# Copying the first batch's split q and k from SBUF straight to the stacks, and moving batch 1's projections and split ahead of other start-up work, in a fused adaLN, attention and mixture-of-experts kernel

## The reference: what is computed

```python
mod = (_silu(L0_c) @ L0_wmod).reshape(L0_c.shape[0], 6, 1, -1)
sa, ca, ga, sb, cb, gb = (mod[:, 0], mod[:, 1], mod[:, 2], mod[:, 3], mod[:, 4], mod[:, 5])
ga = (2 * (ga >= 0) - 1) * jnp.maximum(jnp.abs(ga), 0.25)   # gb in the same way
h = _layernorm(x, axis=-1) * (1 + ca) + sa
x = x + ga * _L0_attn_ref(h, ...)      # 16 heads of width 8, softmax over 256 keys
h = _layernorm(x, axis=-1) * (1 + cb) + sb
x = x + gb * _L0_ffn_ref(h, ...)       # 14 experts, one (the argmax) for each token
```

## Time and profile before

| what | value |
|---|---|
| median of 3 runs | 626.4 us (625.49 to 626.9) |
| the profiled execution, from its first to its last instruction | 626.1 us |
| PE, DVE, ACT, POOL busy | 476.2, 552.7, 543.4, 498.0 us |
| granted PE clock, mean | 0.637 |

### The profile page before, as it was taken

The page is one execution under the profiler, slowest core; times in us unless marked ns, Lnnn a source line. Parts: engine busy times, 40 slices in busy tenths (PEclk is TensorE's granted clock), DMA queues, the critical chain, the costliest instruction groups (busy, mean ns, idle before and its releaser), DMA issues.

```text
span 626.1 us, 11856 instructions
## 1 busy us (share of the span) xinstructions
PE 476.2 (76%) x2529; PEld 269.8 (43%) x2531; DVE 552.7 (88%) x1430; ACT 543.4 (87%) x2310; POOL 498.0 (80%) x655
## 2 busy tenths in 40 slices
PE   5457877887687888787777788788766868989880
PEld 2123333433333333343333344344332548878870
DVE  5899899999999999999999999999999787868660
ACT  2599999999999999999999999999999656757650
POOL 4466777898998999998998989899887664777774
PEclk9556566556756655556656655655655588999886
DMA  6365555555555545554445555655553126676640
GB/s 193 106 184 144 135 136 141 148 149 146 155 151 146 155 139 144 147 148 137 143 135 144 152 158 172 182 164 162 146 156 111 50 90 183 189 205 190 194 124 1
DMA packets 75432, 91.66 MB, mean 146 GB/s; under 512 B 12925, under 2 KB 59043, under 8 KB 75359
## 3 DMA queue, kind: packets, MB, share of 16 engines
q1 hardware_dynamic: 66826, 72.93, 43.6%
q0 software_dynamic: 6560, 16.83, 7.2%
q10 hardware_dynamic: 1976, 1.15, 0.7%
HBM read 58.41 MB, written 33.29 MB: 146 GB/s over the span
## 4 chain that ended last, share of the span: by engine, by line
ACT 47%; POOL 17%; DVE 13%; PE 8%; issue 8%; DMA 5%; ACTq 1%; POOLq 0%; DVEq 0%; SPq 0%
ACT scores L785 46%; DVE neg_max L1218 4%; POOL table L710 3%; PE scores L1052 3%; DMA x_s<-table 2%; POOL xhat L659 2%; PE scores L1061 2%; DMA out_dram<-out_room,ids_s 2%; POOL rstd L642 2%; POOL rest L478 1%; POOL parts L481 1%; POOL out_dram L761 1%; POOL h_scaled L682 1%; DVE w_e L1670 1%; POOL xhat L651 1%
## 5 line engine op out<-in xcount | busy, mean ns | idle before, releaser
L785 ACT ACTIVATE scores<-scores,neg_max 128x256 f32<-128x256 f32 x1024 | 468.5, 864 | 10.9 <-DVE neg_max L1218 10.7
L785 ACT ACTIVATION_READ_ACCUMULATOR scores<-scores,neg_max 128x1 f32 x1024 | 438.3, 624 | 0.0
L1218 DVE TENSOR_REDUCE neg_max<-scores 128x4 f32<-128x1024 f32 x256 | 309.1, 1211 | 6.7 <-PE scores L916 5.9
L916 PE MATMUL scores<-k_stack,q_stack 64*128 64x256 bf16 x1024 | 149.2, 390 | 80.8 <-ACT scores L785 69.2
L916 PEld LDWEIGHTS scores<-k_stack,q_stack 64*128 64x128 bf16 x1024 | 33.9, 106 | 166.1 <-ACT scores L785 121.3
L710 POOL DMA_INDIRECT table<-rows,place_i x64 | 66.1, 1033 | 19.9 <-issue 17.7
L761 POOL DMA_INDIRECT out_dram<-out_room,ids_s x65 | 65.8, 1013 | 19.8 <-issue 15.8
L817 ACT ACTIVATE hid<-scores,w_e 128x128 f32<-128x128 f32 x154 | 48.3, 365 | 22.2 <-PE scores L1052 21.2
L1052 PE MATMUL scores<-x_t,w_e 128*128 128x128 f32 x308 | 52.5, 297 | 1.7 <-ACT x_t L810 1.4
L659 POOL TENSOR_SCALAR xhat<-rows,mv,rstd 128x128 f32<-128x128 f32 x60 | 47.7, 797 | 7.1 <-POOL rstd L642 7.1
L1061 PE MATMUL scores<-w_s,hid 128*128 x308 | 50.1, 288 | 1.1 <-ACT hid L817 0.9
(11 more groups left out here) (178 smaller groups left out, 826.9 us busy)
## 6 DMA issues: line engine op xcount, KB each, us to landing
x_s<-table SPq DMA_DIRECT2D x77, 192.5 KB, 3.0
q_stack<-parts_dram SPq DMA_DIRECT2D x192, 64.0 KB, 2.9
parts_dram<-parts SPq DMA_DIRECT2D x31, 384.0 KB, 3.0
k_stack<-parts_dram SPq DMA_DIRECT2D x186, 64.0 KB, 2.3
mod_b<-mod_rows SPq DMA_DIRECT2D x32, 256.0 KB, 4.3
x_s<-in_x_dram SPq DMA_DIRECT2D x13, 256.0 KB, 4.7
w1x_s<-in_w1x_dram SPq DMA_DIRECT2D x7, 258.0 KB, 4.4
w_s<-in_w_dram SPq DMA_DIRECT2D x7, 256.0 KB, 4.5
```

Source lines behind the costliest of these rows:

```text
L785: last = act.activation(buf[:, k * L:k * L + L], buf[:, k * L:k * L + L], ACT.Exp, bias=neg_max[:, p, n:n + 1], accum_out=exp_sum[:, p, n: ...
L916: last = pe.matmul(scores[:, c, at:at + L], q_stack[p][r, g + j, t * P:t * P + P], k_stack[p][r, g + j, :], start=True, stop=True)
L1218: dve.tensor_reduce(to, scores[:, (PAIRS * b.n + i) % RING, :].rearrange("p (e j m) -> p e j m", e=2, j=2), AX_X, ALU.max, negate=True).th ...
```

## The change

Two things are changed. First, the parts of batch 0 no longer go through `parts_dram`. The new `load_first_by` copies one part of q or k from SBUF to each place of the stack that takes it: 9 DMAs from SP and 3 from ACT, each issued when its part is made. `first_k_stored` falls away, batch 2's split waits for all of stack 0 in its place, and the counts of `parts_stored` fall by one store. Second, the order at the start changes: PE runs the transposes and projections of batch 1 ahead of `late_mod`, DVE takes q and k of batch 1 ahead of `take_mod`, POOL splits batch 1 ahead of `root(3)` and `normalise_x(Batch(2))`, and DVE's `means` of batch 2 moves from ahead of `take_mod` to behind `modulate(0)`.

```diff
--- before.py
+++ after.py
@@ -369,7 +369,6 @@
         first_rest = sem("first_rest")
         first_middle = sem("first_middle")
         first_q_ready = sem("first_q_ready")
-        first_k_stored = sem("first_k_stored")
         b_qk_turned = sem("b_qk_turned")
         b_taken = sem("b_taken")
         w_moe_loaded = sem("w_moe_loaded")
@@ -469,9 +468,9 @@
 
             eng.wait_ge(qk_ready, b.done())
 
-            need(eng, parts_stored, 16 * b.n - 16)
             if b.n == 2:
-                eng.wait_ge(first_k_stored, 16)
+                eng.wait_ge(stacked[0], 16 * LOADS_STACK)
+            need(eng, parts_stored, 16 * b.n - 32)
             p = b.slot(2)
             steps.plain()
             steps.then(eng.tensor_copy(parts[:, p, :, 0, :], qk[:, :, :]))
@@ -488,6 +487,13 @@
                     src = parts_dram[p, side, part].rearrange("(c g) t -> c (g t)", g=HALF)
                     eng.dma_start(to[p][n:P:ROWS, :, :].rearrange("c g t -> c (g t)"), src).then_inc(stacked[p], 16)
 
+        def load_first_by(eng, side, part):
+
+            to, part_of = ((q_stack, Q_PART), (k_stack, K_PART))[side]
+            for n in range(COMBOS):
+                if part_of[n] == part:
+                    eng.dma_start(to[0][n:P:ROWS, :, :], parts[:, 0, side, part, :]).then_inc(stacked[0], 16)
+
         @block.sync
         def _(sp):
             steps = Steps(sp, sp_held, sp_held)
@@ -515,7 +521,7 @@
 
             def parts_landed(b):
 
-                sp.wait_ge(parts_stored, 16 * b.n + 16)
+                sp.wait_ge(parts_stored, 16 * b.n)
                 steps.plain()
 
             def pad_front(n):
@@ -527,11 +533,13 @@
             sp.wait_ge(pad_set, 2)
             pad_front(0)
             sp.wait_ge(stacks_set, 4)
+            for side in range(2):
+                sp.wait_ge(first_high, side + 1)
+                load_first_by(sp, side, 0)
+            sp.wait_ge(first_middle, 1)
+            load_first_by(sp, 0, 1)
             sp.wait_ge(first_q_ready, 1)
-            sp.dma_start(parts_dram[0, 0].rearrange("s r t -> r s t"), parts[:, 0, 0]).then_inc(parts_stored, 16)
-            sp.wait_ge(parts_stored, 16)
-            steps.plain()
-            load_stacks_by(sp, 0, (0,))
+            load_first_by(sp, 0, 2)
             store_parts(Batch(1))
             parts_landed(Batch(1))
             load_stacks_by(sp, 1, (0, 1))
@@ -713,9 +721,9 @@
             root(1)
             root(2)
             normalise_x(Batch(1))
+            split_by(pool, steps, Batch(1))
             root(3)
             normalise_x(Batch(2))
-            split_by(pool, steps, Batch(1))
             pool.wait_ge(w_in_loaded, 16 * LOADS_IN)
 
             def iteration(b):
@@ -858,10 +866,10 @@
             act.copy(first[1][:, 1, :], rest[:, 1, :]).then_inc(first_middle, 1)
             act.wait_ge(stacks_set, 4)
 
+            act.wait_ge(first_middle, 2)
+            load_first_by(act, 1, 1)
             act.wait_ge(parts_ready, 1)
-            act.dma_start(parts_dram[0, 1].rearrange("s r t -> r s t"), parts[:, 0, 1]).then_inc(first_k_stored, 16)
-            act.wait_ge(first_k_stored, 16)
-            load_stacks_by(act, 0, (1,))
+            load_first_by(act, 1, 2)
             over_batches(iteration, drain)
 
             over_tiles(tile, PRIMED, AT_W1)
@@ -985,10 +993,10 @@
             pe.wait_ge(h_ready, 1)
             pe.matmul(first_qk[0], w_qk_s[:, 0, :], h_t[0][:, :], start=True, stop=True).then_inc(first_q_done, 1)
             pe.matmul(first_qk[1], w_qk_s[:, 1, :], h_t[0][:, :], start=True, stop=True).then_inc(qk_done, 1)
-            late_mod()
             turn_x(Batch(1))
             project_q(Batch(1))
             project_k(Batch(1))
+            late_mod()
             pe.wait_ge(b_taken, 1)
 
             pe.wait_ge(mod_taken, 2)
@@ -1379,9 +1387,6 @@
                 dve.tensor_tensor(parts[:, 0, side, 2, :], rest[:, side, :], parts[:, 0, side, 1, :], ALU.subtract).then_inc(done, 1)
             make_h(Batch(1))
             stats_x(Batch(2))
-            dve.wait_ge(xhat1_ready, 2)
-            steps.plain()
-            means(True, False)
             dve.wait_ge(consts_set, SETS)
 
             def take_mod():
@@ -1418,11 +1423,14 @@
                 steps.then(dve.tensor_tensor(bias_out[:, 1, :], bias_f[:, 1, :], bias_f[:, 1, :], ALU.max))
                 dve.tensor_tensor(bias_out[:, 2, :], bias_f[:, 1, :], bias_out[:, 1, :], ALU.subtract).then_inc(bias_ready, 1)
 
+            take_qk(Batch(1))
             take_mod()
-            take_qk(Batch(1))
             dve.wait_ge(mod_taken, 2)
             steps.plain()
             modulate(0)
+            dve.wait_ge(xhat1_ready, 2)
+            steps.plain()
+            means(True, False)
             dve.wait_ge(w_in_loaded, 16 * LOADS_IN)
             dve.wait_ge(mod_taken, 2)
             dve.wait_ge(xhat1_ready, 3)
```

## The result

The changed kernel takes 631.62 us (median of 6 runs, 628.85 to 632.18) against 626.08 for the kernel before in the same comparison: a ratio of 1.0075, 95% interval 1.0055 to 1.0094, that is 4.7 us slower (3.4 to 5.9). In a second comparison it was 631.28 against 626.52, ratio 1.0074 (1.0055 to 1.0092).

The account below looks back on a forecast made before the run. The first exponential, following the first row maximum by 1.26 us, was taken to set the end; DVE's chain through POOL moved that maximum from 20.97 to 24.9. So 626.1 + 3.9 = 630.0, plus 0.3 for the median: 630.3, range 628.4 to 631.4.

Parts of the forecast that it names:

- DVE's chain through POOL: Start: `means` of batch 2 at 20.2, POOL's normalisation, `before_s` at 24.0, first row maximum 24.9 against 20.97, +3.9 us.
- Dearer still: Rival: POOL's last split instruction, 1.15 us, holds up one of DVE's, +5.0, 631.4; or copies land past 24.2; chance 0.07.
- The first exponential sets the end: ACT hardly pauses after its first exponential, at most 0.7 us idle, so moving that moves the kernel's end equally.
- Getting the stacks sooner can therefore be worth 1.3 us and no more.: First row maximum: DVE was held 1.34 us by the scores, its own earlier work ending at 19.62.
- The copies: Batch 0's stack copies: nine on SP at 0.66 us each, the ninth issued by 16.2, landing at 18.5 against 20.19.
- PE at slow pace: Batch 1's projections from 13.1 to 15.2, `late_mod` done at 17.9; slow all through, chance 0.65.
- The term that was mis-sized: `modulate(0)`: DVE's modulation beside POOL's split: four instructions in 1.21 us, ending at 20.16, with a price of at most 0.1.
- The small terms: DVE at the start: `means` straight behind `modulate(0)`, 3.82 us to `before_s`, then 0.84 to the first row maximum.
- POOL's split costs nothing at slow pace: POOL splits batch 1 from 16.0 to 19.85, 0.4 us before `root(3)` can start, so the chain pays nothing.
- The rival of a quicker PE: Projections in 1.12 us and `late_mod` in half of 2.77; first row maximum at 23.3, +2.3, 628.7; chance 0.18.
- Its smaller case: Only `late_mod` is quick on PE; POOL's split ends at 19.85 and the total is +3.3.
- The base: Sum: 626.1 us for the profiled execution plus 3.9 gives 630.0; the runs' median lies 0.3 above, so 630.3.

Follow-up runs that it names:

- no_third_wait: Changed kernel, but ahead of its loop DVE waits for its own statistics of batch 2, not for POOL's normalisation; ratio to the kernel before 1.0016.
- chain_back: Changed kernel with DVE's statistics of batch 2 and POOL's normalisation of it back in their old places; ratio to the kernel before 1.0017.
- order_only: Kernel before with only the new order on PE, DVE and POOL; batch 0 still goes through DRAM; ratio 1.0070, 4.4 us slower.
- late_mod_first: Changed kernel with `late_mod` again ahead of batch 1's transposes and projections on PE, DVE's and POOL's new order kept; ratio to the kernel before 1.0070.
- one_input: Changed kernel, but the first of `modulate(0)`'s DVE instructions reads one SBUF input in place of two, the second two; ratio to the kernel before 1.0074.
- gates_after_split: As `early_split`, but both gates made behind the third and fourth row maxima, `before_s` and `next_row` moved to batch 1; 624.02 us against 626.52, ratio 0.9962.
- early_split_late_gates: As `early_split`, but `before_s` and `next_row` stand ahead of `modulate(0)`; ratio to the kernel before 1.0013.
- early_split: Changed kernel with `late_mod` first on PE, early batch 2 statistics without the wait for POOL, POOL's split between `root(3)` and normalisation; ratio to the kernel before 1.0039.
- copies_only: Changed kernel without its new order, so only batch 0's copies from SBUF to the stacks; ratio to the kernel before 0.9982, in a repeat 0.9988.

## Why the prediction was right, point by point

The prediction said 630.3 us, 3.9 slower than before, with a range up to 631.4 and DVE's chain through POOL as cause. The ratio gives 4.7 (3.4 to 5.9), the start of the exponentials 4.5. The step that carries it is shown: `no_third_wait`, which changes nothing but DVE's wait for POOL, gives back 3.4 us at the start, and so does `chain_back`. The range only just holds. Its upper end was 631.4, and the six runs of the changed kernel have a median of 631.62; by the ratio, from the 626.4 of before, it is 631.1. Inside that time is a term that the main line of the prediction put at 0.1 us at most, the hold described below, which it had only as the rival "Dearer still" with a chance of 0.07.

- **The first exponential sets the end.** Borne out in the large: starts that moved by +4.5, +4.3, +4.5, +4.2, +1.1, +1.1 and -2.6 us gave +4.7, +4.4, +4.4, +4.6, +1.1, +1.0 and -2.4 by the ratios (the changed kernel, `order_only`, `late_mod_first`, `one_input`, `chain_back`, `no_third_wait`, `gates_after_split`). Three runs fit less well: `early_split_late_gates` (+0.15 gave +0.8), `early_split` (+0.6 gave +2.4, beyond its interval), and `copies_only`, which won 1.4 at the start, lost 1.25 at batch 1 and still came out 1.1 faster. So the start predicts the time of a version to about 1 us, with one miss of 1.8 that is not explained.
- **"Getting the stacks sooner can therefore be worth 1.3 us and no more."** Right for the start (1.4 measured). The prediction did not follow it to batch 1, where the trace shows a gap of 1.25; the expectation of `copies_only` did.
- **The copies.** Predicted 0.66 us each on SP and complete at 18.5; measured 0.66 over the nine and, in `copies_only`, 17.85. The landing is counted from the start of an issue, and the prediction had added it to the end of the last one.
- **PE at slow pace.** Predicted 13.1, 15.2 and 17.9 for the start of the projections, their end and the end of `late_mod`; measured 12.94, 15.02 and 17.72. The rule of the Trainium skill that the prediction cites (TensorE: Matmul & The Clock Gate, section What's actually happening), that activity has to release the clock, is in line with the lengths: PE had idled 1.18 us ahead of the projections, and they are slow. But that `late_mod` stays slow as well was partly luck. In the same place it took 2.77 us in both profiles of the changed kernel, and 2.60, 2.51, 2.43 and 2.05 in `chain_back`, `one_input`, `no_third_wait` and `order_only`.
- **The term that was mis-sized: `modulate(0)`.** "Four instructions in 1.21 ... so a price of at most 0.1", and "the trace does not agree" with the Trainium skill (SBUF — State Buffer, section SBUF: two separate sides). It took 2.01 us (18.91 to 20.92), 0.80 more, all of it in one instruction held by POOL's. `one_input`, `chain_back` and `late_mod_first` show the hold. My step from the earlier trace rows was wrong because POOL's instruction beside `modulate(0)` there was a TENSOR_SCALAR, and the one it would meet was a TENSOR_TENSOR. This is the rival "Dearer still", at 0.80 us in place of 1.15. The rows themselves held a sign of it: `before_s` took 0.37 us there and ended at 19.15, 0.07 behind POOL's CAST (18.47 + 0.61), where it takes 0.23 alone. And the trace of before holds such meetings with TENSOR_TENSOR, which I had not looked for. DVE's timeline at 175 us:

```profile
175.67 0.51 DVE L1291 SCALAR_TENSOR_TENSOR first<-below,expert_s 128x56 f32<-128x56 f32 x1
```

  0.51 us where most of its kind take 0.2, ending 0.07 behind a TENSOR_TENSOR of 128x256 on POOL (175.38 + 0.73). It began inside one, with 0.3 us or more of it left, five times in that trace and took 0.39 to 0.72 each time; another with two SBUF inputs, `one_hot<-first,rank_top`, began inside one of 128x512 six times and took 0.71 to 1.07 in place of 0.20.
- **The small terms.** `means` waits 0.28 us for `modulate(0)`'s last result and `modulate(0)` 0.15 for its copies, which I took as nothing; from `means` to the first row maximum it was 4.29 us (21.20 to 25.49) against a predicted 4.7. With `late_mod` 0.18 early these nearly cancel, so that 24.9 + 0.80 is near the measured 25.49, 0.2 above it.
- **POOL's split costs nothing at slow pace.** Its own time did not (it ended at 19.83, predicted 19.85), but it cost through the hold. The rival of a quicker PE, for which I had +2.3 to +3.3, was not met whole by any run. Its smaller case was met in part by `order_only`: with `late_mod` quicker by 0.7 us it was still +4.4 at the first row maximum, since the hold took most of what PE gave (`modulate(0)` took 2.41 us there). So the +3.3, which has no hold in it, is likely too low.
- **The base.** Span and device time differ by 1.8 us, so the sum should have been made as a difference alone. It was, in effect, since it added 3.9 to the median of 626.4, and the error in words did no harm to the number.

## What to carry to other kernels

Ahead of a loop, a wait in one engine's list binds all that the awaited engine does first: before work is moved, list who waits for whom at the seam, and ask whether the wait is for the right event (here the engine's own statistics would have done, and one line was worth 3.4 us at the start). An edit that frees a resource sooner pays only as far as the next arrival, so look at the next two batches too. And small VectorE instructions on two SBUF inputs, and some on one, are best kept away from GpSimd's long TENSOR_TENSORs: moved beside the split, four of 0.28 us, in 1.2 us when alone, took up to 3.4.

## What the runs showed of the hardware

- A DVE instruction with two SBUF inputs that starts while POOL runs a TENSOR_TENSOR of 128x512 or 128x256 ends 0.07 to 0.14 us behind POOL's, whatever its own length (0.28 alone; 1.06, 1.12, 1.20 held). POOL's CAST of 128x512 held such ones too: 0.58 in `chain_back`, 0.55 in `order_only`, 0.74 in `late_mod_first`. Beside POOL's TENSOR_SCALAR of 128x128 four such ran at full speed. The Trainium skill (SBUF — State Buffer, section SBUF: two separate sides) tells of a shared port pair with an exclusive lock, for two SBUF inputs against a GpSimd instruction that reads SBUF. These runs bear out the lock beside TENSOR_TENSOR and CAST, and not beside TENSOR_SCALAR, which reads SBUF as well.
- Of DVE instructions with one SBUF input some were held and some were not. The CAST of 128x128 was (1.04 in place of 0.23). So was a TENSOR_SCALAR, in DVE's timeline of before at 281 us:

```profile
281.38 0.83 DVE L1460 TENSOR_SCALAR early_i<-early_i 77x14 int32<-77x14 int32 x1
```

  It began inside a TENSOR_TENSOR of POOL (281.03 + 1.16) and ended 0.02 behind it; at 512.9 us the same operation takes 0.17. BATCH_NORM_STATS2 was not held (0.49 in `gates_after_split`). What decides between them was not tested.
- A DVE instruction that had begun first was not held, and POOL's paid little: its CAST took 0.67 us in place of 0.61 in `chain_back`, its TENSOR_TENSOR 1.19 and 1.20 in place of 1.15 in `no_third_wait` and `one_input`.
- The granted clock of the records is no guide near the start. The stretches of PE in the changed kernel, with the columns of the earlier trace rows:

```profile
42.00:46.00 4.00, 2.19 (x13) 1.00 0.91 209
46.00:50.00 4.00, 3.42 (x14) 1.00 0.67 217
```

  and its timeline in the second of them:

```profile
46.66 1.06 PE L911 MATMUL side_b<-h_t,w_qk_s 128*128 128x256 f32 x2
```

  The clock is given as 1.00 (2.4 GHz), and the k projection has the 1.06 us that stand in the earlier trace rows for batch 0, not the 0.59 of the quick one.
- Copies of 64 KB from SBUF to SBUF in rows of 512 bytes cost the queue 0.63 to 0.66 us each and land 2.0 to 2.2 us after their issue.
